# A recommendation tower: the first pair of tiles with eight tables by lookups and two by gathers, tile 14's last units turned by TensorE, ScalarE's last moves reordered

## What is computed

```python
e = stack([tbl_f[ids[:, f]] for f in range(26)], axis=1)         # 2048 x 26 x 128
all_emb = concatenate([bottom_output[:, None, :], e], axis=1)    # 27 vectors of 128
gram = einsum('bfd,bgd->bfg', all_emb, all_emb)
z = gram[:, TRIU_I, TRIU_J]                                      # 351 pairs
h = maximum(concatenate([z, bottom_output], axis=1) @ W_top1 + b_top1, 0)   # 479 x 512
h = maximum(h @ W_top2 + b_top2, 0)                                         # 512 x 256
y = h @ W_top3                                                              # 256 x 1
```

## Time and profile before

| | |
|---|---|
| median of 3 runs | 358.29 us (357.15 to 359.43) |
| profiled execution | 361.95 us, of which the span of the instructions is 360.2 us |
| PE busy, PE weight loads busy | 330.1 us (92%), 301.7 us (84%) |
| DVE busy | 268.5 us (75%) |
| ACT busy | 226.0 us (63%) |
| POOL busy | 255.4 us (71%), of it 254.0 in 264 gathers of 0.96 us |
| mean granted PE clock | 0.986 |
| share of DMA engines: SP's transfers, POOL's gathers | 39.2%, 20.4% |

### The profile page before, as it was taken

One profiled execution on the slowest core, in us unless ns is written; L12 is line 12 of the kernel. 1 busy time (PEld: TensorE's weight loads), 2 busy tenths in 40 slices (PEclk: granted clock), 3 DMA queues, 4 the chain that ended last, 5 costly groups with the idle time before them and its releaser, 6 DMA issues.

```text
span 360.2 us, 14054 instructions
## 1 busy us (share of the span) xinstructions
PE 330.1 (92%) x5976; PEld 301.7 (84%) x5976; DVE 268.5 (75%) x805; ACT 226.0 (63%) x357; POOL 255.4 (71%) x274
## 2 busy tenths in 40 slices
PE   0987999589999999998999999999999999978896
PEld 0876989489989999897999999999899899866685
DVE  4999999947769986798688978698787978330412
ACT  5677674467676767665774786666674686653331
POOL 6777777777777777777777777777777777777400
PEclk9999999969999999999999999999999999999899
DMA  7866575465655777768564888559575855555100
GB/s 218 228 175 191 154 249 195 86 150 112 111 127 104 166 115 117 117 146 124 117 140 93 135 147 104 130 107 171 88 150 107 150 124 96 104 87 110 38 4 1
DMA packets 71485, 45.79 MB, mean 127 GB/s; under 512 B 60288, under 2 KB 62976, under 8 KB 71296
## 3 DMA queue, kind: packets, MB, share of 16 engines
q1 hardware_dynamic: 62976, 27.59, 39.2%
q0 software_dynamic: 8448, 17.32, 20.4%
HBM read 31.24 MB, written 0.01 MB: 87 GB/s over the span
## 4 chain that ended last, share of the span: by engine, by line
PE 50%; POOL 18%; DMA 12%; issue 9%; ACT 5%; DVE 4%; SPq 0%; ACTq 0%; DVEq 0%
PE hot_ps L445 18%; POOL X L391 18%; PE gram_ps L424 8%; DMA turned<-planes 6%; PE h_ps L477 6%; PE xt_ps L445 5%; PE h_ps L511 5%; DMA X<-in_table_dram,rows_sb 4%; PE h_ps L474 3%; ACT planes L756 2%; PE xt_ps L405 2%; DVE onehot L634 2%; ACT XT L610 2%; DMA stage_sb<-in_hot_dram 1%; DVE tab L685 1%
## 5 line engine op out<-in xcount | busy, mean ns | idle before, releaser
L391 POOL DMA_INDIRECT X<-in_table_dram,rows_sb x264 | 254.0, 962 | 81.7 <-issue 78.3
L634 DVE TENSOR_SCALAR onehot<-ids_wide,row_value 128x256 fp32r<-128x256 int16 x664 | 207.4, 383 | 43.6 <-PE hot_ps L445 28.4
L445 PE MATMUL hot_ps<-onehot,tab 128*128 128x256 f32 x1000 | 141.8, 295 | 13.0 <-DVE onehot L634 10.6
L445 PEld LDWEIGHTS hot_ps<-onehot,tab 128*128 128x128 f32 x1000 | 130.4, 197 | 16.3 <-issue 12.4
L610 ACT COPY XT<-turned 128x512 int16<-128x512 int16 x104 | 83.0, 879 | 18.8 <-DMA turned<-planes 18.8
L756 ACT COPY planes<-X 128x1024 int16<-128x1024 int16 x52 | 56.0, 1077 | 29.5 <-DMA X<-in_table_dram,rows_sb 27.9
L424 PEld LDWEIGHTS gram_ps<-XT 128*27 128x27 f32 x4096 | 45.9, 105 | 24.1 <-ACT XT L610 9.9
L424 PE MATMUL gram_ps<-XT 128*27 128x26 f32 x4096 | 56.2, 193 | 10.6 <-ACT XT L610 8.3
L766 ACT COPY XT<-hot_ps 128x256 f32<-128x256 f32 x56 | 38.6, 689 | 35.6 <-PE hot_ps L445 35.6
L445 PE MATMUL xt_ps<-onehot,tab 128*128 128x256 f32 x360 | 51.1, 290 | 0.0
L445 PEld LDWEIGHTS xt_ps<-onehot,tab 128*128 128x128 f32 x360 | 46.2, 191 | 0.7
(11 more groups left out here) (45 smaller groups left out, 116.0 us busy)
## 6 DMA issues: line engine op xcount, KB each, us to landing
ids_wide<-in_hot_ids_dram SPq DMA_DIRECT2D x14, 320.0 KB
X<-in_table_dram,rows_sb POOLq DMA_INDIRECT x264
stage_sb<-in_hot_dram SPq DMA_DIRECT2D x15, 256.0 KB, 4.3
stage_sb<-in_hot_dram SPq DMA_DIRECT2D x10, 192.0 KB, 3.6
bottomT<-in_bottom_t_dram SPq DMA_DIRECT2D x8, 128.0 KB, 5.0
w_sb<-in_w_dram SPq DMA_DIRECT2D x1, 1024.0 KB, 7.6
turned<-planes SPq DMA_TRANSPOSE x52
w_sb<-in_w_dram SPq DMA_DIRECT2D x1, 512.0 KB
```

The lines of the kernel that those rows point to most:

```text
L391: pool.indirect_dma_start(X[:, n % RING, k, :], None, table, bass.IndirectOffsetOnAxis(idx[:, column:column + 1], 0)).then_inc(gathered[n ...
L445: mm = pe.matmul(hot_bank(i)[:, 0:WIDE], tab[u][:, part, D * c:D * (c + 1)], onehot[p % ONEHOTS][:, c - PIECE[u][h], :], start=(c == 0 and ...
L634: compared = dve.tensor_scalar(onehot[p % ONEHOTS][:, c - PIECE[u][h], :], ids_wide[:, u, :], row_value[:, c:c + 1], None, ALU.is_equal)
```

## The change

1. `SOMETIMES` goes from 4 to 2, so that `HOT_BASE` is 8: the first pair looks up two more tables of 1250 rows, and two hot tables are left to gathers. Their unit has now two gathers, each of 64 samples by 2 tables (`width(n)`, and the lists of indices on the host), and two PE transposes, and its move copies half as much. There are 260 gathers. Six pieces of tables move from the late splits to the first stage; steps 0 to 5 have one late piece each.
2. Units by DMA are now those of blocks 8 to 56; blocks 57, 58 and 59 of tile 14 become DIRECT. Step 55 moves into `last_blocks()`, with a wait until the lookup in `xt_ps` is placed. PE transposes blocks 57 to 59 there among the grams and layer 1.
3. ACT's steps from 56 on are written out: moves and relus in the order in which PE asks for them, with moves of a block before the relus of the layer 1 columns that PE computes after them.

```diff
-SOMETIMES = 4
+SOMETIMES = 2
-TILE_COLUMNS = BLOCKS * (1 + ALWAYS // FOUR)
+TILE_COLUMNS = SOMETIMES + BLOCKS * (ALWAYS // FOUR)
-DIRECT_TILES = (0, 1, TILES - 1)
-DIRECT = [n for n, (t, j) in enumerate(UNITS) if t in DIRECT_TILES]
-BY_DMA = [n for n, (t, j) in enumerate(UNITS) if t not in DIRECT_TILES]
+TURN_FROM, TURN_TO = 8, LAST + 1
+BY_DMA = [n for b in range(TURN_FROM, TURN_TO) for n in UNITS_OF[b]]
+DIRECT = [n for n in range(len(UNITS)) if n not in BY_DMA]
+def width(n):
+    return SOMETIMES if UNITS[n][1] is None else FOUR
+def landed(n):
+    return 16 * sum(width(m) for m in range(n % RING, n + 1, RING))
...
-                for k in range(FOUR):
+                for k in range(width(n)):
                     pool.indirect_dma_start(X[:, n % RING, k, :], ...)
...
             def last_blocks():
+                b, t = LAST - 1, TILES - 3
+                lookups(*slice_of(b))
+                pe.wait_ge(hot_placed, len(LOOKUPS) - 2)
+                transposes(UNITS_OF[b + 2])
+                gram(b)
+                mlp(t, BLOCKS - 1)
                 b, t = LAST, TILES - 2
                 gram(b)
                 z_transposes(t - 1)
                 gram(b + 1)
+                transposes(UNITS_OF[b + 2])
                 layer1(len(JOBS) - 3, 0)
                 layer1(len(JOBS) - 3, 1)
                 gram(b + 2)
+                transposes(UNITS_OF[b + 3])
                 layer1(len(JOBS) - 3, 2)
...
-            for b in range(LAST):
+            for b in range(LAST - 1):
                 step(b)
             last_blocks()
...
             def step(b):                                  # ACT
-                if t >= TILES - 2:
-                    moves(b + 1)
                 relus(t, j)
...
-                if t < TILES - 2:
-                    moves(b + 1)
+                moves(b + 1)
+            def last_blocks():                            # ACT
+                b = LAST
+                moves(b + 1)
+                moves(b + 2)
+                relu(len(JOBS) - 3, 0)
+                relu(len(JOBS) - 3, 1)
+                moves(b + 3)
+                relu(len(JOBS) - 3, 2)
+                relu(len(JOBS) - 3, 3)
+                place_bottom(TILES - 1)
+                b = LAST + BLOCKS
+                moves(b)
+                moves(b + 1)
+                relu(len(JOBS) - 2, 0)
+                relu(len(JOBS) - 2, 1)
+                moves(b + 2)
...
-            for b in range(TILES * BLOCKS):
+            for b in range(LAST):
                 step(b)
-            for c in range(C1):
-                relu(len(JOBS) - 1, c)
+            last_blocks()
```

More of the change, by code:

```diff
@@ L400, in transposes @@
                     if n in DIRECT:
-                        pe.wait_ge(gathered[n % RING], 16 * FOUR * (n // RING + 1))
+                        pe.wait_ge(gathered[n % RING], landed(n))
                         if NTH[n] > 0:
                             pe.wait_ge(xt_moved, DIRECT[NTH[n] - 1] + 1)
-                        for k in range(FOUR):
+                        for k in range(width(n)):
                             mm = pe.transpose(xt_ps[:, P * k:P * (k + 1)], X[:, n % RING, k, :], ident[:])
@@ L601, in move_turned @@
             eng.wait_ge(turned_in[slot], 16 * (NTH[n] // TURNED + 1))
[L602 to L611, removed]
+            wait(eng, gram_full, BLOCKS * (t - XTILES) + j + 1)
+            for h in range(2):
+                moved = copy(words[:, t % XTILES, PAD * j:PAD * (j + 1), 0:ALWAYS, h].rearrange("d s (k f) -> d s k f", f=FOUR),
+                             turned[:, slot, h::2, :].rearrange("d k (s f) -> d s k f", f=FOUR))
             moved.then_inc(xt_moved, 1)
@@ L752, in split_words @@
                         k = NTH[n]
-                        act.wait_ge(gathered[n % RING], 16 * FOUR * (n // RING + 1))
+                        act.wait_ge(gathered[n % RING], landed(n))
                         if k >= TURNED:
@@ L825, in step @@
                     split_first(q)
-                if t < TILES - 2:
-                    moves(b + 1)
+                moves(b + 1)
[15 more added lines that the diff above has]
+                moves(b + 2)
+                relu(len(JOBS) - 2, 2)
+                relu(len(JOBS) - 2, 3)
+                moves(b + 3)
+                for c in range(C1):
+                    relu(len(JOBS) - 1, c)
             act.memzero(zt_ps[:]).then_inc(zt_pads_zero, 1)
@@ L891 @@
     starts = _np.cumsum([0] + [tables[f].shape[0] for f in listed])[:-1].astype(_np.int32)
-    wanted = ids[sample][:, :, listed].reshape(TILES, BLOCKS, PAD, TILE_COLUMNS // BLOCKS, FOUR)
-    always = wanted[:, :, :, :-1].transpose(2, 4, 0, 1, 3).reshape(P, TILES, ALWAYS)
-    extra = wanted[:, :, :, -1].transpose(2, 3, 0, 1).reshape(P, TILES, BLOCKS)
+    always = ids[sample][:, :, rest].reshape(TILES, BLOCKS, PAD, ALWAYS // FOUR, FOUR)
+    always = always.transpose(2, 4, 0, 1, 3).reshape(P, TILES, ALWAYS)
+    extra = ids[sample][:, :, hot[HOT_BASE:]].reshape(TILES, SOMETIMES, P // SOMETIMES, SOMETIMES)
+    extra = extra.transpose(2, 3, 0, 1).reshape(P, TILES, SOMETIMES)
     columns = _np.concatenate([extra, always], axis=2).reshape(P, TILES * TILE_COLUMNS)
-    lists = starts.reshape(TILE_COLUMNS // BLOCKS, FOUR).T
-    lists = _np.concatenate([_np.repeat(lists[:, -1:], BLOCKS, axis=1), _np.tile(lists[:, :-1], (1, BLOCKS))], axis=1)
-    starts = _np.tile(lists, (PAD, 1))
+    always = _np.tile(starts[:ALWAYS].reshape(ALWAYS // FOUR, FOUR).T, (PAD, BLOCKS))
+    extra = _np.tile(starts[ALWAYS:, None], (P // SOMETIMES, SOMETIMES))
+    starts = _np.concatenate([extra, always], axis=1)
     hot_ids = ids[sample][:, :, hot].reshape(GROUPS, WIDE, HOT).transpose(0, 2, 1).astype(_np.int16)
```

10 lines of the change are left out of this document (2 added, 8 removed).

## The result

| | before | changed |
|---|---|---|
| median of 4 runs each, same chip | 358.59 us (357.15 to 359.43) | 362.76 us (361.5 to 364.91) |
| ratio of the changed kernel | | 1.012 [1.0074, 1.0165] |
| profiled execution, its span | 361.95, 360.2 us | 361.8, 359.9 us |

358.8 us was forecast (356.6 to 361.6), most likely no change. The median is 4 us above that and outside the range: slower by 0.7 to 1.7%. The two profiled executions, however, are level, as the sum said of them.

A forecast was written before the change was run, and what follows sets the result against it. DVE bounds the first stage, PE and POOL the middle, chains of waits the end. Gathers +6.6 us and PE +6.2, against a tail of 27.0 instead of 32.7, give +0.5 on 358.3: 358.8 us, range 356.6 to 361.6.

The forecast's parts named there:

- a table in the first stage: First lookups: each added table of 1250 rows costs full DVE 4.17 us, 8.3 us for two.
- standstill before unit 6: Start: POOL stands 12 us before block 4's unit, waiting for PE to transpose block 1.
- unit 6's gather: Start: the gather for block 4 begins at 42.6, 7.05 us later than before.
- last gather: End of POOL's gathers: starts 6.6 us later than 337.08, at 343.7.
- gram 55: Before the last blocks: PE arrives at block 55 6.2 us later than 316.04.
- gram 55 to 63: Last blocks: PE's work sums to 26.6 us plus 0.4 for small waits, 27.0 against 32.7 before.
- gram 63: Last block: 349.2 by PE, 349.1 by the gathers; the later taken, +0.5 us on 348.75.
- the difference is carried over: Last step: the +0.5 us found for the profiled execution is added to the 358.3 us median, giving 358.8.
- The tail's 5.7 us: Last blocks: gain from PE transposing blocks 57 to 59 without DMA transposes, 32.7 us becoming 27.0.
- A: Start: PE turns block 1 in time, POOL isn't held, gathers 5.0 us earlier; 352.6 us; chance 0.13.
- B: Last blocks: PE waits for landing or ACT, the 32.7 us stay; 364.5 us; chance 0.17.
- C: Middle: PE has reserve and catches up to POOL's pace, last gather sets the end; 358.7 us; chance 0.10.

The follow-up runs named there:

- second comparison: The unedited changed kernel timed again beside the kernel before on one chip: 362.46 us against 360.45, ratio 1.0096.
- last blocks alone: Parts 2 and 3 of the change on the kernel before, with SOMETIMES still 4: 356.45 us against 360.45, ratio 0.9927.
- less PE work: 65 of the last pair's second-part lookup products left out: changed kernel 361.6 us, ratio to before 1.0075; kernel before 358.8 us, 1.0024.
- block 1 turned earlier: Changed kernel with only block 1's unit transposed behind the sixth first-stage table, ACT's move with it: 360.03 us against 360.68 for before, 1.0005.
- turned early: Changed kernel with blocks 1, 2, 3 transposed in the first stage and tile 1's units one step sooner: 356.06 us against 360.45 for before, 0.9893.
- turned early, row broken: Kernel with all first units transposed early, plus DVE waiting for its own last piece before each of six one-hot pieces: 354.44 us, 0.9839 to before.

## Why the prediction was wrong

Its steps, against the profile of the changed kernel:

| step | forecast | measured |
|---|---|---|
| a table in the first stage | 4.17 us | 3.9 |
| standstill before unit 6 | 12 us | 11.93 |
| unit 6's gather | 42.6 | 41.90 |
| last gather | 343.7 | 343.10 |
| gram 55 | 322.2 | 321.54 |
| gram 55 to 63 | 27.0 us | 26.94 |
| gram 63 | 349.2 | 348.48 |
| span | 360.7 | 359.9 |
| median | **358.8** | **362.76** |

**The step that failed is the last one**: "the difference is carried over". The sum described one execution of before with a late PE and compared it with the changed kernel; +0.5 us is near for that pair of executions, measured -0.3. It was then set on a median that other executions of before make. The span forecast, with the 1.75 us that lie outside the span before, was 362.45 us, and that number is right to 0.3 us (362.76, and 362.46 in the second comparison), in part by luck: the changed kernel's profiled execution took 361.8 us. The 3.7 us by which the profiled execution stood above the median were a warning: most executions of before ended sooner, and the gain of the tail was sized on one that didn't. That profiling itself adds such a time is a rival that no run excludes for this kernel; the profiled executions of the other kernels on such chips stood from 1.3 us below to 3.6 us above their medians, so it doesn't do so in general. The range had the same fault and a smaller one: of the 1.1 us for the spread its high end got 0.2, and with all of it, at 362.5, it would still have missed.

**Which term is mis-sized by this.** The tail's 5.7 us. It is 5.8 in profiles where PE arrives at 316 us or later, and 2.6 to 4.0 in time (last blocks alone). Part 1 costs the 6 us that it was given (the changed kernel against the last blocks alone). Why the tail gives less in time is argued here, not shown, with an earliest end for either kind of tail, worked out from rows:

- After the change in the tail, gram 63 can't be earlier than the last gather + 2.5 to 3.8 us of landing (less PE work, block 1 turned earlier) + 1.35. With 11.4 us from gram 63 to the end of the span (359.9 - 348.48) and 1.8 outside it the earliest end is last gather + 17.1 to 18.4, and 19.3 where the end is slow as with block 1 turned earlier.
- Before, grams 56 and 57 hang on gathers through ACT's split, a DMA transpose and a move, so that a part of PE's early arrival is lost: 344.60 - 337.51 = 7.1 us from last gather to gram 63 with PE 7 us early, and the earliest end is last gather + 20.3. This figure comes from one profile, and in it PE doesn't wait for the last unit.

| kernel | last gather | gram 63 behind it, in the profile | earliest end | fastest execution | median |
|---|---|---|---|---|---|
| changed again | 342.9 | 6.6 | 360.0 to 361.3 | 360.8 | 362.5 |
| changed, less PE work | 343.2 | 3.9 | 360.3 to 361.6 | 359.6 | 361.6 |
| block 1 turned earlier | 341.2 | 5.1 | 358.3 to 359.6 | 358.4 | 360.0 |
| before | 336.4 to 337.1 | 14.4, 11.7 | 356.7 to 357.4 | 355.6 | 359.2 to 360.5 |
| last blocks alone | 336.6 | 7.9 | 353.7 to 355.0 | 353.8 | 356.5 |
| turned early | 335.1 | 10.4 | 352.2 to 353.5 | 353.8 | 356.1 |
| turned early, row broken | 333.1 | 9.3 | 350.2 to 351.5 | 352.7 | 354.4 |

The fastest executions lie from 1.1 us below these bounds to 1.2 us above them, so the bounds are estimates and not limits, and the medians stand 0.6 to 3.6 us above their middle. By this account the change moves the last gather by 6.0 us and lowers what has to come behind it by 20.3 - 17.7 = 2.6: +3.4 us (2.8 to 5.0 with 17.1 and 19.3), where the medians differ by 4.2 and 2.0 us and the ratios are 1.012 and 1.0096. An earliest end set by the last gather was first held against the runs with less PE work: it forecast the changed kernel's 361.6 us rightly and a gain of 2 to 5 us for the kernel before wrongly. The 20.3 us were put in after that, and no further run tested the account. Only two profiles show PE waiting for the last unit, block 1 turned earlier and less PE work. In those of the last three kernels of the table gram 63 comes 7.9 to 10.4 us behind the last gather, where landing and transposes need some 4 to 5: in them PE and not the gather sets the end.

The forecast had the gather's path at 349.1 against PE's 349.2, with a landing of 4.1 us from the earlier trace rows. Measured landings, where PE waited, are 2.5 and 3.8: the two paths were further apart than it said, by 0.3 to 1.6 us, and still near enough that 5.5 us less of PE's way brought only 2.5 us in gram 63 and 0.9 in the median. The chance of slower, 0.18, rested on the tail giving nothing; that the tail gives all in the profile and half to two thirds of it in time was in no rival.

**The rivals.** A (POOL not held) fell: 11.93 us. Its time of 352.6 is not the measured one, but its mechanism was right, as the early-turned kernels show with 356.1 and 354.4. B (the tail gives nothing) fell: 26.94 us, with no wait of PE in its timeline. C (PE catches up) fell in the middle: grams 27 and 55 of the changed kernel stand at 175.88 and 321.54, 41.6 us a pair, as before; but that the last gather can set the end was right once PE arrives early, as two profiles show.

```profile
175.88 0.88 PE L434 MATMUL gram_ps<-XT 128*27 128x26 f32 x64
```

**What stays open.** How the usual execution of before gets to its end: no profile of one was taken. And why PE loses time in blocks 8 to 12 in one execution and less in another: 3.4 us lie between the two profiles of before at gram 12, 2.5 us between those of the changed kernel (99.19, 101.66). The windows show the granted clock low (0.66 to 0.83) after waits for landed units. In both kernels with the units turned early it is 1.00 there, and the mean clock of all their executions is 0.990 or more, where those of before go down to 0.972; that speaks for units that land sooner as the cure, with one profile a kernel.

## What to carry to other kernels

When the profiled execution stands above the median, a difference read from it need not hold for the median: work out for each path to the end an absolute time (last gather + landing + what follows; PE's arrival + tail), take the later of them for either kernel, and ask which of them the shorter executions of before are on. A ring slot that is given back in PE's program order ties the gathering engine to that order; where work is added to a first stage, turn landed units within it, which here made +1.0% into -1.1% (-1.6% with the row of one-hots broken, though the two intervals overlap).

## What the runs showed of the hardware that was not expected

A gather that POOL has under way beside an unbroken row of DVE one-hots (int16 in, fp32r out, 256 columns, 0.267 us each) lasts until just behind the row's end: 7.79 us beside 27 one-hots, 4.98 us beside 20, where 0.95 is usual. That is seen in two kernels on the 360 us chip and in one of them on the 627 us chip. The kernel before has it on the latter too, beside a row of 11 at 0.270 us each:

```profile
46.46 2.97 DVE L634 TENSOR_SCALAR onehot<-ids_wide,row_value 128x256 fp32r<-128x256 int16 x11
45.55 4.01 POOL L391 DMA_INDIRECT X<-in_table_dram,rows_sb  x1 [3.08 <-PE xt_ps L405]
```

With DVE waiting for itself between pieces of three or four one-hots (0.321 us each, 8.66 us for 27) the gathers beside it stay at 0.94 to 1.03 us, and the row costs 1.5 us more; this edit alone took the long gather away. In the kernel before on the 360 us chip a row of 27 took 8.34 us (0.309 each) and the gathers beside it stayed at 0.94; why that row is slower and leaves POOL alone was not found.

Landing of the last unit, from the start of its last gather, took 2.51 and 3.79 us, where the middle of the kernel showed 4.1 and 5.0.
